# A gated cross-attention block on one core: moments and features of the score tiles handed to ScalarE and GpSimd

## The chip, the core and the metric

The kernel runs on one core of one Trainium2 chip. A core has TensorE (PE in the profile), VectorE (DVE), ScalarE (ACT), GpSimd (POOL) and the queue engine SyncE (SP), each with an instruction stream of its own that runs strictly in order; they meet only at semaphores. The metric is the device time of one launch in microseconds, the median of several runs.

## The reference

The inputs are x and a context, both (8, 512, 512) in float32. For each of the 8 batches the block computes an attention with 16 heads of width 32, whose temperature is computed from the scores themselves, and then a feed-forward part with quantised weights and activations:

```
Q, K, V = LN(x) @ Wq.T + bq, ctx @ Wk.T + bk, ctx @ Wv.T + bv        # 16 heads
scores  = Q K^T / sqrt(32)
mean_sim = mean(scores); max_sim = mean over rows of max(scores)
entropy_proxy = mean over rows of var(softmax(scores), ddof=1)
t    = exp(clip(MLP([mean_sim, max_sim, entropy_proxy])))              # one per head
attn = softmax(Q K^T / (2 t)) V
x    = x + tanh(g0) * (attn @ Wo.T + bo)
x    = x + tanh(g1) * (quant(gelu(quant(LN(x)) @ quant(W1).T)) @ quant(W2).T)
```

So the scores of a head are needed twice: once for the three features (called pass A below), and once, divided by the temperature, for the attention itself (pass B).

## The kernel before, in words

**Tiles.** A batch has 16 heads x 4 row blocks = 64 score tiles of 128 x 512 in pass A. Tile k belongs to head k // 4 and row block k % 4. Each goes through four steps: TensorE makes the scores in one of four PSUM banks (`a_ps`, `score_a`, L1471); VectorE takes minus the row maximum (`nmax`, `row_max`, L1007); ScalarE takes the exponential into one of three buffers (`etile`, `first_exp`, L778); VectorE takes the moments of that with a BN_STATS instruction (`stat`, `row_stat`, L1017), two tiles later. TensorE may write tile k when the exponential of tile k - 4 is done. For a few tiles of the first and of the last turn that has a pass A (`by_act`), ScalarE makes the moments: its exponential also sums the row (an accumulator read follows), and a Square with a sum (`square`, L788) follows the next exponential; VectorE then leaves out its BN_STATS for this tile and completes the six numbers of `stat` later (`stats_by_act`).

**Turns.** `body(i, par)` runs for i = -1 to 8; i = 1 to 6 are a loop of three passes over two bodies. In such a turn the core works on three batches at once: pass A of batch i, pass B and the feed-forward part of batch i - 1, and the projections K, V and Q of batch i + 1. Within a turn the order of the stages on every engine is the same:

1. the score section: 16 sets of pass B with 40 of the 64 pass-A tiles between them;
2. the four K products (`split_product`, 12 matmuls each, into the banks `b_ps0`, `b_ps1`, `o_ps`, `z_ps`), then the four products with Wo ("W"), the turned x ("X"), three V products, and the four Q products. The 24 remaining pass-A tiles stand beside these. How many stand where is written out in `A_PLAN`: the tuple has 16 places, four each for K, W, V and Q;
3. the features of pass A (`features`, on VectorE: sums and differences over `stat`, a reciprocal, and reductions over `nmax`, 12 small instructions), and the feed-forward part: the up products in row blocks t (`up`, L1650), Gelu by ScalarE (`gelus`, L940), the row maximum and the quantisation by VectorE (`scale_h`, L1218, and `quantise_h`, L1235), the turn of the quantised rows by TensorE (`turn`, L1661), half of which VectorE takes out of PSUM (`turned_h`, L1244), and the down products (L1685). After the up products of block 2 TensorE multiplies the features (L1720, L1724).

Four PSUM banks are taken in rotation by all products; `take` waits until the bank's last content has been taken out.

**What couples K and W.** ScalarE takes each K product out of its bank twice (`qk_out`: L847 with a sum, L851 in float16), after the exponentials of the pass-A tiles that stand beside this product. GpSimd then makes the float16 remainder of K product n (`split_qk(n)`, L684), and behind the one of n = 1 it scales and splits the last quarter of the attention's result (`split_y`: L640, L643, L645), whose last step signals `y_done`. TensorE waits for `y_done` before the first W product.

Of the kernel before, what the change touches and what calls it, by code (L numbers as in the profile page):

```python
# [22 lines left out]
ALU = mybir.AluOpType  # L23
# [43 lines left out]
BY_ACT = {b: sum(by_act(b, k) for k in range(H * T)) for b in (0, 7)}  # L67
# [3 lines left out]
LINKS_END = 12  # L71
LOWEST = -3.0e38
BIAS_STEPS = 5
SETUP_STEPS = G4 + 6
# [108 lines left out]
def nth(b, per, k):  # L183


    return (b + 1) * per + k
# [37 lines left out]
def flamingo_kernel(nc, x, ctxT, g_xattn, g_ffn, WqT, bq, WkT, bk, WvT, bv, WoT, bo,  # L224
                    w1T, b1, w2T, b2, w3T, b3, f1T, f2T, out):
    with ExitStack() as ctx:
# [3 lines left out]
        def sem(name):  # L230
            return ctx.enter_context(nc.semaphore(name))
# [58 lines left out]
        qmask = sb("qmask", [P, G4])  # L290
# [113 lines left out]
        qk_lo_done = per_batch("qk_lo_done", 2 * C)  # L404
        m_link = per_batch("m_link", LINKS_M)
        feat_done = per_batch("feat_done", 1)
        logt_done = per_batch("logt_done", 1)
        expt_done = per_batch("expt_done", 1)
        inv2t_done = per_batch("inv2t_done", 1)
# [3 lines left out]
        def slot_of(n):  # L413
            return (n % G4) * C + n // G4
# [171 lines left out]
        def _(pool):  # L586
            pool_waits = Waits(pool, stood)
            for s, events in per.values():
                pool.sem_inc(s, events)
            pool.sem_inc(out_done, 16 * T)  # L590
            for n in range(UNUSED):
                pool.sem_inc(mm_full[n], 1)
                pool.sem_inc(mm_free[n], 1)
# [78 lines left out]
            def from_cin(n):  # L672
                return cin[:, n % 2, :]


            def body(i, par):
# [65 lines left out]
        def _(act):  # L742
# [37 lines left out]
                                     accum_out=stat[:, at, 1:2] if by_act(b, k) else None).then_inc(a_exp, 1)  # L780

            def squares_by(b, k):
                return (BY_ACT[0] if b > 0 else 0) + sum(by_act(b, n) for n in range(k + 1))

            def square(b, k):
                at = slot_of(k // T) * T + k % T
# [197 lines left out]
        def _(dve):  # L984
            dve_waits = Waits(dve, stood)
            vec = nc.vector
# [30 lines left out]
                vec.bn_stats(stat[:, slot_of(k // T) * T + k % T, :], etile[:, k % E_SLOTS, :]).then_inc(a_stat, covered)  # L1017

            def stats_by_act(i):
                if i == 0:  # L1020
                    by_tile = stat[:, :, :].rearrange("p (g c t) f -> p g c t f", g=G4, t=T)
                    own = by_tile[:, :, 1:3, T - 1, :]
                else:
                    by_tile = stat[:, :, :].rearrange("p (h t) f -> p h t f", t=T)
                    own = by_tile[:, 2 * C - 1::C, :, :]
                mean, mean_too, rest = (own[:, :, :, f] for f in (1, 4, 5))
                links = 2 if i > 0 else 0
                dve_waits.wait_ge(squared, BY_ACT[0] + (BY_ACT[7] if i > 0 else 0))
                vec.tensor_scalar(mean, mean, 1.0 / S, None, ALU.mult).then_inc(act_link, 1)
                dve_waits.wait_ge(act_link, links + 1)  # L1030
# [3 lines left out]
                dve_waits.wait_ge(act_link, links + 2)  # L1034

            def tile_a(b, k, looked=False):

# [26 lines left out]
            def features(b, par):  # L1064
# [242 lines left out]
            def body(i, par):  # L1307
# [473 lines left out]
```

## Time and profile before

| | |
|---|---|
| median of 3 runs | 1333.83 us (1332.42 to 1334.48) |
| profiled execution, device time | 1336.35 us |
| its span, first to last instruction | 1334.5 us |
| mean granted TensorE clock | 0.969 |
| busy: PE / DVE / ACT / POOL | 89% / 82% / 71% / 30% of the span |
| chain that ended last, by engine | PE 49%, DVE 26%, issue 10%, ACT 8% |

The turns i = 1 to 7 end, by the temperature's last step on VectorE, at 316.4, 469.5, 623.7, 776.8, 930.8, 1083.9 and 1221.7 us. So a turn of the loop is 153.1 to 154.2 us long, and the six of them repeat one pattern. In the turn that ends at 623.7 us the score section runs to 539.8 us, the K products to 552, W to 564, X and V to 576, Q to 590, and the feed-forward part from 590. A row of the timeline gives the start and the duration in us, the engine and line, the tiles, and in brackets how long the engine had been idle before, and for whom it had waited. Durations of neighbouring instructions overlap in their last 0.1 us, so the pitch from start to start is what an engine needs for each.

### The profile page before, as it was taken

The numbers are of one execution on the slowest core, as the hardware profiler recorded it, in microseconds if no ns is written. First come the engines' busy times: TensorE is split into PE (matmuls) and PEld (weight loads), VectorE is DVE, ScalarE is ACT, GpSimd is POOL, SyncE is SP. The second block draws the span as 40 slices with busy tenths as digits, with TensorE's granted clock in tenths as the row PEclk, the third lists the DMA queues.
The fourth block names the chain that finished last, engine by engine and source line by source line (L and its number), as shares of the span: only waits on it lengthen the run. The fifth ranks groups of instructions, "written<-read, shape, count | busy, mean of one in ns | idle before, by whom it ended". The sixth has DMA issues, their size and how long they took to land.

```text
span 1334.5 us, 23561 instructions
## 1 busy us (share of the span) xinstructions
PE 1186.8 (89%) x6684; PEld 439.0 (33%) x6684; DVE 1093.2 (82%) x2049; ACT 941.7 (71%) x1593; POOL 396.3 (30%) x387
## 2 busy tenths in 40 slices
PE   4866598989999999998999999999989899869988
PEld 2322221444134422444124431344214441224234
DVE  7789689896998869896998869897898979985256
ACT  4688598576985689575985669665985669765833
POOL 3138555311452024510353124510353101100120
PEclk9969799999999999999999999999999999979989
DMA  8722211221112221211112221102112210001000
GB/s 305 224 75 64 55 41 49 48 48 58 35 39 48 57 74 48 49 38 42 50 48 48 55 76 49 28 21 65 64 49 48 48 65 1 1 0 47 18 0 32
DMA packets 36049, 73.70 MB, mean 55 GB/s; under 512 B 8144, under 2 KB 8528, under 8 KB 35408
## 3 DMA queue, kind: packets, MB, share of 16 engines
q1 hardware_dynamic: 35920, 72.13, 18.8%
q8 instruction: 62, 1.02, 0.3%
q14 instruction: 67, 0.55, 0.1%
HBM read 38.39 MB, written 8.39 MB: 35 GB/s over the span
## 4 chain that ended last, share of the span: by engine, by line
PE 49%; DVE 26%; issue 10%; ACT 8%; SPq 2%; DMA 1%; DVEq 1%; ACTq 0%; POOL 0%; POOLq 0%
PE b_ps L1445 10%; DVE stat L1017 7%; PE o_ps L1685 6%; DVE nmax L1007 5%; PE o_ps L1490 4%; ACT region L810 4%; PE o_ps L1445 4%; PE b_ps L1477 4%; PE a_ps L1471 4%; PE z_ps L1445 3%; ACT etile L778 2%; DVE hmax L1218 2%; PE z_ps L1685 2%; PE z_ps L1501 2%; PE b_ps L1650 2%
## 5 line engine op out<-in xcount | busy, mean ns | idle before, releaser
L778 ACT ACTIVATE etile<-a_ps,nmax 128x512 f32<-128x512 f32 x512 | 369.1, 734 | 104.3 <-DVE nmax L1007 104.1
L810 ACT ACTIVATE region<-b_ps,inv2t 128x512 f32<-128x512 f32 x512 | 354.8, 758 | 50.0 <-PE b_ps L1477 46.1
L1007 DVE TENSOR_REDUCE nmax<-a_ps 128x1 f32<-128x512 f32 x512 | 345.9, 679 | 53.7 <-PE a_ps L1471 49.7
L1017 DVE BATCH_NORM_STATS2 stat<-etile 128x6 f32<-128x512 f32 x492 | 335.5, 685 | 15.5 <-ACT etile L778 15.2
L1471 PE MATMUL a_ps<-kst,qst 96*128 96x512 f16 x512 | 198.1, 390 | 32.1 <-ACT etile L778 25.5
L1477 PE MATMUL b_ps<-qst,kst 97*128 97x512 f16 x512 | 192.8, 389 | 23.6 <-DVE region L1244 7.7
L1490 PE MATMUL o_ps<-region,vbuf 128*32 128x512 f32 x1024 | 137.2, 608 | 10.9 <-ACT region L810 7.1
L1477 PEld LDWEIGHTS b_ps<-qst,kst 97*128 97x128 f16 x512 | 49.2, 96 | 290.4 <-ACT region L810 259.3
L1501 PE MATMUL z_ps<-region,ones 128*32 128x512 f32 x1024 | 136.2, 604 | 8.4 <-DVE region L1054 8.4
L684 POOL TENSOR_TENSOR region<-region 128x512 f16<-128x512 f32 x64 | 79.8, 1249 | 208.9 <-ACT region L851 208.9
L640 POOL TENSOR_TENSOR region<-region 128x512 f32<-128x512 f32 x32 | 40.9, 1280 | 285.4 <-DVE region L1061 285.4
L1218 DVE TENSOR_REDUCE hmax<-region 128x1 f32<-128x512 f32 x128 | 81.7, 680 | 12.1 <-ACT region L940 10.9
L613 POOL CAST c_hi<-cin 128x512 f16<-128x512 f32 x28 | 17.1, 611 | 243.8 <-DMA cin<-in_ctxT_dram 243.0
L1685 PE MATMUL o_ps<-f,region 128*128 128x512 fp8e4 x352 | 79.6, 379 | 0.0
L1650 PE MATMUL b_ps<-f,region 128*128 128x512 fp8e4 x256 | 65.1, 394 | 15.2 <-DVE region L1244 12.1
L1471 PEld LDWEIGHTS a_ps<-kst,qst 96*128 96x128 f16 x512 | 50.7, 99 | 80.7 <-ACT etile L778 44.9
L940 ACT ACTIVATE region<-b_ps,xmax 128x512 f32<-128x512 f32 x64 | 43.3, 689 | 27.9 <-PE b_ps L1650 27.6
L661 POOL TENSOR_SCALAR cin<-cin,mv,rstd 128x512 f32<-128x512 f32 x28 | 58.1, 2081 | 2.8 <-POOL rstd L652 2.6
L950 ACT ACTIVATE region<-b_ps 128x1024 f16<-128x1024 f16 x31 | 31.7, 1023 | 31.6 <-PE b_ps L1661 30.8
L1051 DVE TENSOR_SCALAR region<-o_ps 128x512 f32<-128x512 f32 x32 | 21.8, 681 | 37.0 <-PE o_ps L1490 37.0
L650 POOL TENSOR_SCALAR rstd<-mv 128x2 f32<-128x2 f32 (+1 forms) x25 | 5.8, 232 | 139.0 <-DVE mv L1367 52.5
L1685 PEld LDWEIGHTS o_ps<-f,region 128*128 128x128 f16 x352 | 33.8, 98 | 38.1 <-issue 1.1
(313 smaller groups left out, 1989.9 us busy)
## 6 DMA issues: line engine op xcount, KB each, us to landing
kst<-region SPq DMA_DIRECT2D x96, 128.0 KB, 2.3
qst<-region SPq DMA_DIRECT2D x84, 128.0 KB, 2.3
xres<-in_x_dram SPq DMA_DIRECT2D x8, 1024.0 KB, 6.1
out_dram<-xres SPq DMA_DIRECT2D x32, 256.0 KB, 2.0
cin<-in_ctxT_dram SPq DMA_DIRECT2D x30, 256.0 KB, 2.7
cin<-in_x_dram SPq DMA_DIRECT2D x28, 256.0 KB, 2.6
kst<-in_f1T_dram SPq DMA_DIRECT2D x2, 1024.0 KB, 11.5
qst<-in_f2T_dram SPq DMA_DIRECT2D x2, 1024.0 KB, 9.0
```

Source lines behind the costliest of these rows:

```text
L778: nc.scalar.activation(etile[:, k % E_SLOTS, :], a_ps[k % A_BANKS][:, :], ACT.Exp, bias=nmax[:, slot_of(n), t:t + 1], scale=1.0, accum_out ...
L810: nc.scalar.activation(probs[:, (s + 1) % 2, g, :], b_ps[g % 2][:, :], ACT.Exp, scale=inv2t[:, slot:slot + 1]).then_inc(b_exp, 1)
L1007: vec.tensor_reduce(nmax[:, slot_of(k // T), k % T:k % T + 1], a_ps[k % A_BANKS][:, :], AX.X, ALU.max, negate=True).then_inc(a_max, 1)
L1017: vec.bn_stats(stat[:, slot_of(k // T) * T + k % T, :], etile[:, k % E_SLOTS, :]).then_inc(a_stat, covered)
L1218: ins = vec.tensor_reduce(hmax[:, n:n + 1], hbuf[t % 2][:, n * S:(n + 1) * S], AX.X, ALU.max, apply_absolute_value=True)
L1445: ins = mat(mm_ps[bank_n][:, :], left[l](c), right[r](c), start=(c, l, r) == pairs[0], stop=bias is None and (c, l, r) == pairs[-1])
L1471: mat(a_ps[k % A_BANKS][:, :], qst[par][0:SHIFT, slot, t * P:(t + 1) * P], kst[par][0:SHIFT, slot, :], start=True, stop=True).then_inc(a_f ...
L1477: mat(b_ps[g % 2][:, :], kst[par][0:SHIFT + 1, slot, k * P:(k + 1) * P], qst[par][0:SHIFT + 1, slot, :], start=True, stop=True).then_inc(b ...
L1490: ins = mat(o_ps[g * DK:(g + 1) * DK, :], vbuf[par][:, k, n * DK:(n + 1) * DK], probs[:, (s + 1) % 2, g, :], start=k == 0, stop=k == T - 1)
L1501: ins = mat(z_ps[g * DK:(g + 1) * DK, :], ones32[:, 0:DK], probs[:, (s + 1) % 2, g, :], start=k == 0, stop=k == T - 1)
L1650: ins = mat(mm_ps[bank_n][:, :], xqT[:, c, t * P:(t + 1) * P], f1[:, c, n * S:(n + 1) * S], start=c == 0, stop=c == C - 1)
L1685: ins = mat(mm_ps[bank_n][:, :], hT[t % 2][:, k, :], f2[:, k, :], start=k == 0, stop=k == KC - 1)
```

## The change

Four things are edited:

- `A_PLAN`, the places of 24 pass-A tiles in turns 1 to 6: K gets 3, 3, 2, 2 instead of 2, 2, 2, 2; W gets 2, 1, 1, 1 instead of 1, 1, 1, 1; V gets 0, 0, 0, 1 instead of 1, 1, 1, 1; Q keeps 2, 2, 2, 2.
- In turns 1 to 6 ScalarE makes the moments of the odd row blocks of heads 10 and 11, that is of tiles 41, 43, 45 and 47, all of which stand beside the K products.
- In turns 1 to 7 the features are made by GpSimd in 13 linked steps, but for the reciprocal, which stays on VectorE (`inverse_total`). Two steps (the total of `stat` and its square) stand ahead of the last `split_qk`, the rest behind it. The products of the sums of Q and K and the completion of ScalarE's moments stand ahead of the remainders of Q.
- The first turn keeps its plan and its features on VectorE; turn 7 keeps its plan.

```diff
-A_PLAN = (40, (2, 2, 2, 2, 1, 1, 1, 1, 1, 1, 1, 1, 2, 2, 2, 2))
+A_PLAN = (40, (3, 3, 2, 2, 2, 1, 1, 1, 0, 0, 0, 1, 2, 2, 2, 2))
+BY_ACT_HEADS = (10, 11)
 def by_act(i, k):
-    return isinstance(i, int) and (i == 0 and k % T == T - 1 and C <= k // T < 3 * C or i == 7 and k >= H * T - 3 * T)
+    n, row = k // T, k % T
+    if isinstance(i, int) and i == 0:
+        return row == T - 1 and C <= n < 3 * C
+    if isinstance(i, int) and i == 7:
+        return n >= H - 3
+    return n in BY_ACT_HEADS and row % 2 == 1
...
+            def stats_by_act(i):
...
+                mean, mean_too, rest = (own[:, :, :, f] for f in (1, 4, 5))
+                pool_waits.wait_ge(squared, nth(i, BY_ACT[1], count))
+                pool.tensor_scalar(mean, mean, 1.0 / S, None, ALU.mult).then_inc(act_pool, 1)
...
+                pool.tensor_copy(mean_too, mean)
+                pool.tensor_tensor(rest, mean, mean, ALU.mult).then_inc(act_pool, 1)
...
+                pool.tensor_scalar(rest, rest, -float(S), None, ALU.mult).then_inc(act_pool, 1)
...
+            def feature_total(b, c):
+                total = mstep[:, 0, :]
+                pool_waits.wait_ge(a_stat, nth(b, H * T, H * T))
+                if isinstance(b, int) and b == 7:
+                    stats_by_act(b)
+                c.link(pool.tensor_tensor(total, stat[:, :, 1], stat[:, :, 4], ALU.add))
+                c.link(pool.tensor_tensor(total, total, total, ALU.mult))
+            def feature_rest(b, c):
...
+                c.link(pool.tensor_tensor(some, nmax[:, :, 0:2], nmax[:, :, 2:4], ALU.add))
+                c.link(pool.tensor_tensor(feat[:, 1, :], some[:, :, 0], some[:, :, 1], ALU.add))
+                c.link(pool.tensor_tensor(diff, stat[:, :, 1], stat[:, :, 4], ALU.subtract))
+                c.link(pool.tensor_tensor(diff, diff, diff, ALU.mult))
...
+                pool_waits.wait_ge(inv_done, nth(b, 1, 1))
+                c.link(pool.tensor_tensor(square, square, inv, ALU.mult))
...
+                pool.tensor_tensor(feat[:, 2, :], some[:, :, 0], some[:, :, 1], ALU.add).then_inc(feat_done, 1)
...
-                if has_p:
-                    for n in range(C, 2 * C):
-                        split_qk(n)
+                if has_a and has_b:
+                    c = Chain(pool_waits, pool_link, LINKS_POOL, i)
+                    feature_products(i, par, c)
+                for n in range(C, 2 * C) if has_p else ():
+                    if has_a and has_b and n == 2 * C - 1:
+                        feature_total(i, c)
+                    split_qk(n)
+                if has_a and has_b:
+                    if not has_p:
+                        feature_total(i, c)
+                    feature_rest(i, c)
...
+            def inverse_total(b):
+                dve_waits.wait_ge(pool_link, nth(b, LINKS_POOL, 4))
+                vec.reciprocal(mstep[:, 3, :], mstep[:, 0, :]).then_inc(inv_done, 1)
...
-                if has_a and isinstance(i, int) and i == 7:
-                    stats_by_act(i)
-                if has_a:
+                if has_a and has_b:
+                    inverse_total(i)
+                elif has_a:
                     features(i, par)
```

ScalarE in turn 1, from the last exponential but one ahead of the first K product's exit to the second K product's exit; `b_ps0` and `b_ps1` hold the two products, `etile,stat<-` is an exponential or a square that also sums. Before:

```order
L778 ACTIVATE etile<-a_ps3,nmax 128x512
L778 ACTIVATE etile<-a_ps0,nmax 128x512
L118 ISA
L847 ACTIVATE region2,qksum0<-b_ps0,bqk 128x512
L851 ACTIVATE region2<-b_ps0,bqk 128x512
L778 ACTIVATE etile<-a_ps1,nmax 128x512
L778 ACTIVATE etile<-a_ps2,nmax 128x512
L847 ACTIVATE region2,qksum0<-b_ps1,bqk 128x512
L851 ACTIVATE region2<-b_ps1,bqk 128x512
```

The same place of the changed kernel:

```order
L862 ACTIVATE etile<-a_ps3,nmax 128x512
L862 ACTIVATE etile<-a_ps0,nmax 128x512
L862 ACTIVATE etile,stat<-a_ps1,nmax 128x512
L128 ISA
L932 ACTIVATE region2,qksum0<-b_ps0,bqk 128x512
L936 ACTIVATE region2<-b_ps0,bqk 128x512
L862 ACTIVATE etile<-a_ps2,nmax 128x512
L873 ACTIVATE etile,stat<-etile 128x512
L862 ACTIVATE etile,stat<-a_ps3,nmax 128x512
L862 ACTIVATE etile<-a_ps0,nmax 128x512
L873 ACTIVATE etile,stat<-etile 128x512
L932 ACTIVATE region2,qksum0<-b_ps1,bqk 128x512
L936 ACTIVATE region2<-b_ps1,bqk 128x512
```

Ahead of the second K product's exit there are now two more exponentials and two squares; one of the exponentials stands ahead of the first exit.

VectorE after the last pass-A tile of the same turn, with the row maxima of the first feed-forward block (`hmax<-region4`) at the end. Before:

```order
L1017 BN_STATS stat<-etile 128x6
L1069 TENSOR_TENSOR mstep<-stat 128x64
L118 ISA
L1070 TENSOR_TENSOR mstep<-stat 128x64
L1071 TENSOR_TENSOR mstep<-mstep 128x64
L1072 TENSOR_TENSOR mstep<-stat 128x64
L1073 SCALAR_TENSOR_TENSOR mstep<-mstep 128x64
L1075 TENSOR_TENSOR mstep<-mstep 128x64
L1076 RECIPROCAL mstep<-mstep 128x64
L1077 TENSOR_TENSOR mstep<-mstep 128x64
L1078 TENSOR_TENSOR qkprod<-qksum1 128x4
L1079 TENSOR_TENSOR feat<-qkprod,qmask 128x16
```

Three more rows (L1082, L1083 and the first L1218) follow there. In the changed kernel:

```order
L1102 BN_STATS stat<-etile 128x6
L1102 BN_STATS stat<-etile 128x6
L128 ISA
L1170 RECIPROCAL mstep<-mstep 128x64
L1303 TENSOR_REDUCE hmax<-region4 128x1
```

Eleven of the twelve instructions have left VectorE, and the one that stays waits for two steps of GpSimd.

GpSimd behind the remainder of the third Q product (`region1<-region2,region1` is such a remainder) in the changed kernel; before, the last remainder followed the third at once and nothing followed it:

```order
L760 TENSOR_TENSOR region1<-region2,region1 128x512
L128 ISA
L725 TENSOR_TENSOR mstep<-stat 128x64
L726 TENSOR_TENSOR mstep<-mstep 128x64
L760 TENSOR_TENSOR region1<-region2,region1 128x512
L734 TENSOR_TENSOR mstep<-nmax 128x32
L735 TENSOR_TENSOR feat<-mstep 128x16
L736 TENSOR_TENSOR mstep<-stat 128x64
L737 TENSOR_TENSOR mstep<-mstep 128x64
L739 TENSOR_SCALAR mstep<-mstep 128x64
L740 TENSOR_TENSOR mstep<-stat 128x64
L743 TENSOR_TENSOR mstep<-mstep 128x64
```

Three more steps (L745, L747 and L748) end the chain.

## Rows read from the trace of the kernel before

**Rows 1.** Timeline of TensorE, third turn of the loop: first instruction of the W products.
```profile
552.16 0.39 PE L1471 MATMUL a_ps<-kst,qst 96*128 96x512 f16 x1
```

**Rows 2.** Timeline of GpSimd, same turn, from the second K remainder on.
```profile
547.54 1.16 POOL L684 TENSOR_TENSOR region<-region 128x512 f16<-128x512 f32 x1 [1.81 <-ACT region L851]
548.65 1.27 POOL L640 TENSOR_TENSOR region<-region 128x512 f32<-128x512 f32 x1
...
550.78 1.16 POOL L645 TENSOR_TENSOR region<-region 128x512 f16<-128x512 f32 x1
```

**Rows 3.** Timeline of TensorE in the feed-forward part of the same turn.
```profile
600.72 1.07 PE L1661 MATMUL b_ps<-ident,region 128*128 128x128 f16 x16 [0.20 <-DVE region L1235]
...
606.01 1.02 PE L1650 MATMUL b_ps<-f,region 128*128 128x512 fp8e4 x4 [1.63 <-DVE region L1244]
```

**Rows 4.** Timeline of VectorE, same turn, from the last moments to the quantisation.
```profile
589.83 1.87 DVE L1017 BATCH_NORM_STATS2 stat<-etile 128x6 f32<-128x512 f32 x3
...
592.35 1.07 DVE L1071 TENSOR_TENSOR mstep<-mstep 128x64 f32<-128x64 f32 x1
...
595.93 2.46 DVE L1218 TENSOR_REDUCE hmax<-region 128x1 f32<-128x512 f32 x4
...
599.31 1.29 DVE L1235 TENSOR_SCALAR region<-region,hsc 128x2048 f32<-128x2048 f32 x1
```

**Rows 5.** Timeline of ScalarE beside the K products, same turn.
```profile
542.55 0.69 ACT L778 ACTIVATE etile<-a_ps,nmax 128x512 f32<-128x512 f32 x1 [3.35 <-DVE nmax L1007]
543.13 0.68 ACT L847 ACTIVATE region<-b_ps,bqk 128x512 f32<-128x512 f32 x1
...
544.37 0.69 ACT L778 ACTIVATE etile<-a_ps,nmax 128x512 f32<-128x512 f32 x1
...
546.11 0.68 ACT L847 ACTIVATE region<-b_ps,bqk 128x512 f32<-128x512 f32 x1
...
546.77 0.69 ACT L851 ACTIVATE region<-b_ps,bqk 128x512 f16<-128x512 f32 x1
```

**Rows 6.** Timeline of ScalarE in turn 7: exponentials and a square that sum.
```profile
1167.14 0.68 ACT L778 ACTIVATE etile<-a_ps,nmax 128x512 f32<-128x512 f32 x1
...
1167.81 0.62 ACT L788 ACTIVATE etile<-etile 128x512 f32<-128x512 f32 x1
...
1168.42 0.68 ACT L778 ACTIVATE etile<-a_ps,nmax 128x512 f32<-128x512 f32 x1
```

**Rows 7.** Timeline of VectorE beside the K products, third turn: two row maxima.
```profile
542.95 0.67 DVE L1007 TENSOR_REDUCE nmax<-a_ps 128x1 f32<-128x512 f32 x1
...
545.93 0.67 DVE L1007 TENSOR_REDUCE nmax<-a_ps 128x1 f32<-128x512 f32 x1
```

**Rows 8.** One turn earlier, VectorE: the row maximum of tile 41.
```profile
388.52 0.68 DVE L1007 TENSOR_REDUCE nmax<-a_ps 128x1 f32<-128x512 f32 x1
```

**Rows 9.** One turn earlier, ScalarE: the second exit of the second K product.
```profile
392.57 0.68 ACT L851 ACTIVATE region<-b_ps,bqk 128x512 f16<-128x512 f32 x1
```

**Rows 10.** The chain that ended last, in order of time: start us, us, what.
```profile
541.50 0.22 PE a_ps L1471
```

**Rows 11.** Timeline of ScalarE, third turn: the first Gelu.
```profile
593.28 0.69 ACT L940 ACTIVATE region<-z_ps,xmax 128x512 f32<-128x512 f32 x1
```

**Rows 12.** Timeline of GpSimd, third turn: a small step, and the last Q remainder.
```profile
567.15 0.24 POOL L650 TENSOR_SCALAR rstd<-mv 128x4 f32<-128x4 f32 x1 [8.75 <-DVE mv L1367]
...
592.04 1.30 POOL L684 TENSOR_TENSOR region<-region 128x512 f16<-128x512 f32 x1 [1.88 <-ACT region L851]
```

**Rows 13.** Timeline of ScalarE in turn 7: the last Gelu of block 1.
```profile
1199.12 0.69 ACT L940 ACTIVATE region<-z_ps,xmax 128x512 f32<-128x512 f32 x1 [0.17 <-PE z_ps L1650]
```

**Rows 14.** Timeline of VectorE in turn 7: the step behind the maxima of block 1.
```profile
1201.24 0.16 DVE L1221 TENSOR_REDUCE hsc<-hmax 128x1 f32<-128x4 f32 x1
```

**Rows 15.** Timeline of TensorE in turn 0: the restart after a gap.
```profile
102.41 0.39 PE L1471 MATMUL a_ps<-kst,qst 96*128 96x512 f16 x1 [2.50 <-ACT etile L778]
```

**Rows 16.** Busy time by stretch: us, PE, PEld, DVE, ACT, POOL, granted clock, DMA share, GB/s.
```profile
112.00:116.00 4.00, 4.00 (x13) 1.45 (x12) 4.00 (x6) 2.73 (x7) 4.00 (x3) 0.62 0.92 207
```

More of the change, by code:

```diff
@@ L59 @@
 EARLY = A_BANKS
+BY_ACT_HEADS = (10, 11)
 def by_act(i, k):
-    return isinstance(i, int) and (i == 0 and k % T == T - 1 and C <= k // T < 3 * C or i == 7 and k >= H * T - 3 * T)
-BY_ACT = {b: sum(by_act(b, k) for k in range(H * T)) for b in (0, 7)}
+    n, row = k // T, k % T
[4 more added lines that the diff above has]
+    return n in BY_ACT_HEADS and row % 2 == 1
+BY_ACT = {b: sum(by_act(b, k) for k in range(H * T)) for b in (0, 1, 7)}
+assert BY_ACT[0] == 2 * BY_ACT[1]
 assert all(sets + sum(dense) == H * T for sets, dense in (A_PLAN_0, A_PLAN, A_PLAN_7))
@@ L71 @@
 LINKS_END = 12
+LINKS_POOL, LINKS_ACT = 13, 3
 LOWEST = -3.0e38
@@ L406, in flamingo_kernel @@
         feat_done = per_batch("feat_done", 1)
+        pool_link, inv_done, act_pool = sem("pool_link"), sem("inv_done"), sem("act_pool")
         logt_done = per_batch("logt_done", 1)
@@ L590, in _ @@
             pool.sem_inc(out_done, 16 * T)
+            pool.sem_inc(pool_link, 2 * LINKS_POOL)
+            pool.sem_inc(inv_done, 2)
+            pool.sem_inc(act_pool, 2 * LINKS_ACT)
             for n in range(UNUSED):
@@ L673, in from_cin @@
                 return cin[:, n % 2, :]
+            def stats_by_act(i):
+                by_tile = stat[:, :, :].rearrange("p (h t) f -> p h t f", t=T)
+                if isinstance(i, int) and i == 7:
+                    own, count = by_tile[:, 2 * C - 1::C, :, :], BY_ACT[7]
+                else:
+                    first, second = (slot_of(n) for n in BY_ACT_HEADS)
+                    own, count = by_tile[:, first:second + 1:second - first, 1::2, :], BY_ACT[1]
+                mean, mean_too, rest = (own[:, :, :, f] for f in (1, 4, 5))
+                pool_waits.wait_ge(squared, nth(i, BY_ACT[1], count))
+                pool_waits.stand()
+                pool.tensor_scalar(mean, mean, 1.0 / S, None, ALU.mult).then_inc(act_pool, 1)
+                pool_waits.wait_ge(act_pool, nth(i, LINKS_ACT, 1))
+                pool_waits.stand()
+                pool.tensor_copy(mean_too, mean)
+                pool.tensor_tensor(rest, mean, mean, ALU.mult).then_inc(act_pool, 1)
+                pool_waits.wait_ge(act_pool, nth(i, LINKS_ACT, 2))
+                pool_waits.stand()
+                pool.tensor_scalar(rest, rest, -float(S), None, ALU.mult).then_inc(act_pool, 1)
+                pool_waits.wait_ge(act_pool, nth(i, LINKS_ACT, 3))
@@ new lines, in feature_products @@
+            def feature_products(b, par, c):
+                pool_waits.wait_ge(qk_done, nth(b, 2 * C, 2 * C))
+                c.link(pool.tensor_tensor(qkprod[:, :], qksum[par][:, 0:C], qksum[par][:, C:2 * C], ALU.mult))
+                c.link(pool.tensor_tensor(feat[:, 0, :].rearrange("p (g c) -> p g c", g=G4),
+                                          qkprod[:, :].unsqueeze(1).broadcast_to([P, G4, C]),
+                                          qmask[:, :].unsqueeze(2).broadcast_to([P, G4, C]), ALU.mult))
+                if not (isinstance(b, int) and b == 7):
+                    stats_by_act(b)
@@ new lines, in feature_total @@
+            def feature_total(b, c):
+                total = mstep[:, 0, :]
+                pool_waits.wait_ge(a_stat, nth(b, H * T, H * T))
+                if isinstance(b, int) and b == 7:
+                    stats_by_act(b)
+                c.link(pool.tensor_tensor(total, stat[:, :, 1], stat[:, :, 4], ALU.add))
+                c.link(pool.tensor_tensor(total, total, total, ALU.mult))
+            def feature_rest(b, c):
+                total, diff, square, inv = (mstep[:, k, :] for k in range(4))
+                by_tile = square.rearrange("p (h t) -> p h t", t=T)
+                pool_waits.wait_ge(a_max, nth(b, H * T, H * T))
+                some = diff[:, 0:2 * H].rearrange("p (h t) -> p h t", t=2)
+                c.link(pool.tensor_tensor(some, nmax[:, :, 0:2], nmax[:, :, 2:4], ALU.add))
+                c.link(pool.tensor_tensor(feat[:, 1, :], some[:, :, 0], some[:, :, 1], ALU.add))
+                c.link(pool.tensor_tensor(diff, stat[:, :, 1], stat[:, :, 4], ALU.subtract))
+                c.link(pool.tensor_tensor(diff, diff, diff, ALU.mult))
+                pool_waits.stand()
+                c.link(pool.tensor_scalar(diff, diff, S / 4.0, None, ALU.mult))
+                pool.tensor_tensor(square, stat[:, :, 2], stat[:, :, 5], ALU.add).then_inc(pool_link, 1)
+                c.n += 1
+                pool_waits.wait_ge(pool_link, c.base + c.n)
+                c.link(pool.tensor_tensor(square, square, diff, ALU.add))
+                pool_waits.wait_ge(inv_done, nth(b, 1, 1))
+                c.link(pool.tensor_tensor(square, square, inv, ALU.mult))
+                some = total[:, 0:2 * H].rearrange("p (h t) -> p h t", t=2)
+                c.link(pool.tensor_tensor(some, by_tile[:, :, 0:2], by_tile[:, :, 2:4], ALU.add))
+                pool.tensor_tensor(feat[:, 2, :], some[:, :, 0], some[:, :, 1], ALU.add).then_inc(feat_done, 1)
+                c.end()
@@ L782, in squares_by @@
             def squares_by(b, k):
-                return (BY_ACT[0] if b > 0 else 0) + sum(by_act(b, n) for n in range(k + 1))
+                own = sum(by_act(b, n) for n in range(k + 1))
+                return own if isinstance(b, int) and b == 0 else nth(b, BY_ACT[1], own)
             def square(b, k):
@@ L1019, in stats_by_act @@
             def stats_by_act(i):
[L1020 to L1025, printed above, removed]
+                by_tile = stat[:, :, :].rearrange("p (g c t) f -> p g c t f", g=G4, t=T)
+                own = by_tile[:, :, 1:3, T - 1, :]
                 mean, mean_too, rest = (own[:, :, :, f] for f in (1, 4, 5))
-                links = 2 if i > 0 else 0
-                dve_waits.wait_ge(squared, BY_ACT[0] + (BY_ACT[7] if i > 0 else 0))
+                dve_waits.wait_ge(squared, BY_ACT[0])
                 vec.tensor_scalar(mean, mean, 1.0 / S, None, ALU.mult).then_inc(act_link, 1)
-                dve_waits.wait_ge(act_link, links + 1)
+                dve_waits.wait_ge(act_link, 1)
                 vec.tensor_copy(mean_too, mean)
```

2 lines of the change are left out of this document (1 added, 1 removed).

## The prediction

> **What bounds the kernel now.** I read the chain by engine first (PE 49%, DVE 26% of the span), then the waits of TensorE, then the timelines of one loop turn, engine by engine. Six turns repeat one pattern and make up most of the span, so whatever the change does counts six times, and once more in turn 7. In the stretch from the K products to the Q products TensorE issues almost without a gap, and the chain runs along it. VectorE and ScalarE matter there only where TensorE stands still. Two places of the turn are of interest.
>
> The first is the start of the W products at 552.16 [rows 1]. TensorE could not start them before `y_done`, and GpSimd's last step for it ended at 550.78 + 1.16 = 551.94 [rows 2], 0.22 earlier. So this chain is the one that ends last already now, with nothing to spare: ScalarE's second exit of the second K product (546.77 [rows 5]), the remainder at 547.54, the scaling at 548.65, the split to 551.94. The reader should see in rows 2 and 5 that GpSimd starts 0.77 after that ScalarE instruction starts, and was idle before.
>
> The second is the feed-forward part. TensorE waits 0.20 for the first quantised block and 1.63 for the bank that VectorE empties at L1244 [rows 3]. VectorE gets there late since it runs the twelve feature instructions from 591.7 (589.83 + 1.87) to 595.93 before its first maximum of the feed-forward part [rows 4], though the first Gelu is out at 593.28 + 0.69 = 593.97 [rows 11].
>
> **What is gained: the features leave VectorE.** What stays is the reciprocal, behind two GpSimd steps over 64 columns. The trace has no such step. Its nearest rows are 0.24 us for 4 columns and 1.30 us for 512 columns [rows 12]. Between them lies some 0.35, nearer to the small one by its columns; with a link of 0.1 the two steps take 0.9 and the reciprocal, estimated at 0.6 from the 4.2 us that twelve instructions take, ends at about 593.3. That is ahead of the Gelu, so the maxima start at 594.0 instead of 595.93: 1.93 earlier. At the upper end, 1.4 a step, the reciprocal would end at 595.1 and the gain be 0.8; at the lower, 0.25 a step, nothing more is gained, since the Gelu is then last. Everything VectorE does from there to L1244 is its own queue, so the bank comes free up to 1.93 earlier, and TensorE, which idled 0.20 + 1.63 = 1.83 (a little more with the overlap of the rows), can use practically all of it. What is late next is TensorE itself, which has no gap then up to the last turned block. A further bit is lost, because the ten steps of `feature_rest` (ten times 0.45 us from about 594 on, to 598.5) run beside VectorE's first quantisation. The instruction L1071 took 1.07 us [rows 4], and ended when GpSimd's remainder that had begun at 592.04 ended (593.34 [rows 12]); the other feature instructions of its size are far shorter, as the whole chain of twelve takes 4.2. So a VectorE instruction can be held until a GpSimd step ends; one or two such holds of up to 0.35 lie in the path, and I take off 0.23. Gain: 1.7 us a turn, with 0.8 and 1.93 as ends.
>
> Advanced Engine Details and Errata of the Trainium skill, in VectorE Performance Modes, says that GpSimd instructions and VectorE instructions in a two-port mode block each other. The 1.07 us of L1071 agrees with it, and it speaks against this part of the change: before, one GpSimd instruction stood beside the features, now ten stand beside the maxima and the quantisation. By that rule each quantisation that falls into the chain waits at most for the rest of one step, which leaves the sum as it is.
>
> `feat_done` itself is not needed before TensorE's products with the features, right behind the instruction at 606.01 (604.1 then), 5.6 us after the estimated end of the chain. The last Q remainder moves behind the two steps, some 0.7 later; the loads that it releases on the SyncE queue are needed by the engines only some ten us later. In turn 7 the gain is smaller, for there the last Gelu of block 1 ends at 1199.12 + 0.69 = 1199.81 [rows 13]; one maximum (0.69) behind it lets the next step start at 1200.55 instead of 1201.24 [rows 14]: 0.65 gained. The four GpSimd steps for ScalarE's moments that stand ahead there are hidden by this.
>
> **What is lost: ScalarE beside the K products.** Up to the end of the second K product's exit ScalarE has now two more exponentials and two squares with a sum, one of the exponentials ahead of the first exit. Counted out, the pitches are a plain exponential 0.58 (542.55 to 543.13), a K product's exit 1.24 (543.13 to 544.37), its first half 0.66 (546.11 to 546.77) [rows 5]; an exponential with a sum 0.67, a square with a sum 0.61 [rows 6]. The exponential of tile 40 stays at 542.55, as VectorE's maximum sets it. That of tile 41 may start 0.81 after its maximum (542.95 [rows 7]; the same distance that tile 40's has), at 543.76, and must now be done ahead of the first exit: the exit starts at 543.76 + 0.67 = 544.43 and ends at 545.67. Then 0.58 + 0.61 + 0.67 + 0.58 + 0.61 = 3.05 bring the second exit to 548.72 (the maximum of tile 43, at 545.93 [rows 7], is in time, since the moments of tile 41 have left VectorE). Its second half starts at 549.38 instead of 546.77: 2.6 later. One turn earlier the same count from 388.52 [rows 8] gives 389.33 + 0.67 + 1.24 + 3.05 + 0.66 = 394.95, against 392.57 [rows 9]: 2.4 later. The turns alternate between the two patterns, so 2.5 on average. GpSimd, and with it `y_done`, follows by the full amount, since it was idle before the remainder. W starts 2.5 later in each turn. TensorE would be done with the K products at about 552.4, two tiles later than now, and stands still for 2.3 us.
>
> Part of this comes back at once. A tile costs TensorE 0.22 [rows 10]. Behind the start of W it now has one tile more in W and three fewer in V; the two that went to K are done in time that would be idle. That is 2 x 0.22 = 0.43 saved. The four BN_STATS that leave VectorE, at 0.6 each, lie beside TensorE's products and gain nothing; neither does the quantisation of x, which has no tiles in front of it any more and finishes some 2 us earlier, long before TensorE turns it. ScalarE has caught up by the third W product, where it had idled.
>
> The lower end of the loss is 2.1, if the squares overlap more than in turn 7; the upper 3.0, if GpSimd meets the port of VectorE on the way.
>
> **Sum.** A turn: 2.5 - 0.43 - 1.7 = +0.37 us; six turns +2.2; turn 7 -0.65. Together +1.6 us. The profiled execution took 1336.35 us, its span 1334.5 and 1.85 around it; it becomes 1337.9. The median of the runs shown is 1333.83, so I expect 1335.4 there. A change of under 0.2% (2.7 us) is about what a measurement of this kernel cannot tell from none.
>
> **The rivals.** *Faster, A:* the delay at W does not come. ScalarE's order is written, so for that `y_done` would have to be released by something else, or the K products' exits wait less than I count. For it speaks that ScalarE idles 3.35 us ahead of 542.55 [rows 5]; against it that this wait is for VectorE's maximum, and cannot be used. The time would be 6 x (-1.7 - 0.2) - 0.65, that is -12 us: 1322. If only half of the delay comes, it is 1328.
>
> *Slower, B:* the GpSimd chain is slow. Its place is `inverse_total`: VectorE stands at it until GpSimd has done two steps, and behind it are all maxima. At the 1.4 us a step of the upper end the gain falls from 1.7 to 0.8, which costs 6 x 0.9 = 5.4 us more: 1341. If ten such steps end after TensorE needs the features, it waits again: 593.9 + 14 = 608 against 604, another 6 x 4 = 24. It decides from 1.0 us a step on. Against it: the small step of 0.24 us [rows 12].
>
> *Slower, C:* TensorE's clock. The new gap at W is 2.3 us. After a gap of 2.50 us in turn 0 TensorE restarted with 0.39 us a matmul, its fast level of 2.4 GHz [rows 15]; but after further gaps close by the granted clock was 0.62 over 4 us [rows 16], a loss of 0.38 x 4 = 1.5 us at 1.2 GHz. In each turn that would be 6 x 1.5 = +9: 1344. Against it: TensorE is busy without a gap for 12 us on both sides.
>
> **How the numbers follow.** Forecast (both terms as counted, within about 4 us) 0.60; A in whole or part 0.20; B 0.12; C 0.08. The forecast's own range is 1331.5 to 1340: the terms' ends are 2.1 - 0.43 - 1.93 = -0.26 a turn and 3.0 - 0.43 - 1.3 = +1.27. The whole range reaches to half of A and to C's foot: 1327 to 1342. Of the forecast's 0.60, 0.05 is faster by over 0.2%, 0.33 within, 0.22 slower. With A 0.20 faster but for 0.02, and B and C slower but for 0.02, that is faster 0.24, same 0.37, slower 0.39.
>
> **What the profile after must show.** TensorE ahead of the first W product: a gap of about 2.3 us in each of the six turns, and GpSimd's L684 equivalent for the second K product some 2.5 us later against the start of K. TensorE's 1.63 us wait for VectorE's turned block: down to under 0.4. The maxima of block 0 directly behind the first Gelu. GpSimd's steps over 64 columns: 0.3 to 0.4 us. The start of Q after the start of K: 2.1 us later. I am wrong if the W gap stays at 0.2, if steps take 1 us, or if the granted clock in the loop is under 1.00.

## The result

Slower by 0.39%: 1338.07 us median (1334.94 to 1340.72, 8 runs) against 1332.88 (1331.44 to 1334.48, 8 runs), ratio 1.0039, 95% interval 1.0027 to 1.005. On another chip it was 1336.54 (1333.16 to 1342.21, 12 runs) against 1333.09, ratio 1.0028 (1.0014 to 1.0041). The time lies in the predicted range, 2.7 us above the predicted value: +5.2 us were measured where +1.6 were forecast. The runs spread over 5.8 us instead of 3.0. The profiled execution took 1337.47 us (span 1335.7, granted clock 0.967).

### The profile page after: what moved, and what is told of

It reads as the page before. It is cut to its first block, busy times and chain, and to the rows that moved or that the text cites. A ratio compares the mean times of both kernels' runs of the same rounds, so it can differ in the third digit from the quotient of the medians.

```text
span 1335.7 us, 23792 instructions
## 1 busy us (share of the span) xinstructions
PE 1187.1 (89%) x6684; PEld 438.9 (33%) x6684; DVE 1059.5 (79%) x1945; ACT 957.2 (72%) x1665; POOL 433.3 (32%) x513
## 4 chain that ended last, share of the span: by engine, by line
PE 46%; DVE 23%; issue 12%; ACT 11%; SPq 3%; POOL 2%; DMA 2%; DVEq 1%; ACTq 1%; POOLq 0%
PE b_ps L1530 8%; DVE stat L1102 6%; PE o_ps L1770 6%; DVE nmax L1092 6%; PE o_ps L1575 4%; ACT region L895 4%; PE b_ps L1562 4%; PE o_ps L1530 4%; ACT etile L862 3%; PE z_ps L1530 3%; PE a_ps L1556 3%; PE b_ps L1735 2%; PE z_ps L1770 2%; PE z_ps L1586 2%; PE b_ps L1746 2%
## 5 line engine op out<-in xcount | busy, mean ns | idle before, releaser
L1102 DVE BATCH_NORM_STATS2 stat<-etile 128x6 f32<-128x512 f32 x468 | 318.4, 683 | 19.7 <-ACT etile L862 19.4
L760 POOL TENSOR_TENSOR region<-region 128x512 f16<-128x512 f32 x64 | 76.3, 1192 | 196.7 <-ACT region L936 195.3
```

## The profile after

Timeline of TensorE, third turn, the first instruction of the W products, the same place as [rows 1]. The square brackets hold the idle time ahead of it and what ended it.
```profile
555.34 0.39 PE L1556 MATMUL a_ps<-kst,qst 96*128 96x512 f16 x1 [2.13 <-POOL region L659]
```
The gap that was forecast as 2.3 us is 2.13 here and 1.97 in every second turn. GpSimd in the same turn, against [rows 2]: both K remainders, then the scaling and the last step of the split.
```profile
546.42 1.16 POOL L760 TENSOR_TENSOR region<-region 128x512 f16<-128x512 f32 x1 [5.60 <-ACT region L936]
550.70 1.16 POOL L760 TENSOR_TENSOR region<-region 128x512 f16<-128x512 f32 x1 [3.12 <-ACT region L936]
551.82 1.28 POOL L654 TENSOR_TENSOR region<-region 128x512 f32<-128x512 f32 x1
...
553.96 1.16 POOL L659 TENSOR_TENSOR region<-region 128x512 f16<-128x512 f32 x1
```
GpSimd idles 3.12 us for ScalarE, makes the second remainder, and only then starts on y, whose input VectorE had ready at 546.60. ScalarE, against [rows 5]:
```profile
543.12 0.69 ACT L862 ACTIVATE etile<-a_ps,nmax 128x512 f32<-128x512 f32 x1 [3.35 <-DVE nmax L1092]
544.31 0.69 ACT L862 ACTIVATE etile<-a_ps,nmax 128x512 f32<-128x512 f32 x1 [0.50 <-DVE nmax L1092]
...
549.91 0.71 ACT L936 ACTIVATE region<-b_ps,bqk 128x512 f16<-128x512 f32 x1
```
From the first exponential to the second exit's second half it takes 6.79 us, where it took 4.22.

The feed-forward part of the third turn, VectorE first, against [rows 4].
```profile
592.54 1.87 DVE L1102 BATCH_NORM_STATS2 stat<-etile 128x6 f32<-128x512 f32 x3
595.28 0.55 DVE L1170 RECIPROCAL mstep<-mstep 128x64 f32<-128x64 f32 x1 [0.87 <-POOL mstep L726]
596.71 2.46 DVE L1303 TENSOR_REDUCE hmax<-region 128x1 f32<-128x512 f32 x4 [0.87 <-ACT region L1025]
...
600.10 1.29 DVE L1320 TENSOR_SCALAR region<-region,hsc 128x2048 f32<-128x2048 f32 x1
```
Twelve feature instructions have become one reciprocal, and the maxima wait for the first Gelu and no longer for the features. GpSimd beside it:
```profile
594.49 0.38 POOL L725 TENSOR_TENSOR mstep<-stat 128x64 f32<-128x64 f32 x1 [1.62 <-DVE stat L1102]
594.95 0.29 POOL L726 TENSOR_TENSOR mstep<-mstep 128x64 f32<-128x64 f32 x1
...
600.26 1.20 POOL L748 TENSOR_TENSOR feat<-mstep 128x16 f32<-128x16 f32 x1
```
A step over 64 columns takes 0.29 to 0.39 us. Next, the row of the up-projections in the page of the profile, first after the change and then before it. Behind the bar stand busy us, mean ns of one, and the idle us ahead of them with what ended most of it:
```profile
L1735 PE MATMUL b_ps<-f,region 128*128 128x512 fp8e4 x256 | 64.7, 392 | 6.1 <-DVE region L1329 3.3
```
```profile
L1650 PE MATMUL b_ps<-f,region 128*128 128x512 fp8e4 x256 | 65.1, 394 | 15.2 <-DVE region L1244 12.1
```
The wait for the block that VectorE turns out of PSUM [rows 3] has gone from 12.1 us in all to 3.3.

What the prediction gave too little weight shows in the windows of 8 us from the start of W. The last three numbers of a row are the granted clock, the DMA share and GB/s. First and third turn after:
```profile
246.00:254.00 8.00, 7.65 (x28) 3.18 (x29) 4.53 (x7) 4.37 (x9) 5.81 (x7) 0.79 0.43 98
...
555.00:563.00 8.00, 7.67 (x36) 3.50 (x37) 5.72 (x9) 4.37 (x9) 5.81 (x7) 1.00 0.36 82
```
In the first turn TensorE started 28 matmuls instead of 36 and ran at 1.2 GHz for a part of the window (0.21 x 8 = 1.7 us lost). That is called a fall of the clock below. In the other five windows after the change, and in all six before it, the clock was 1.00.

All traces are read by three distances, each worked out from TensorE's timeline as a mean over the six loop turns, in us. "K to W" goes from the first matmul of the K products to the first of the W products (one score tile, 0.22 us, behind the row shown above), "W to up" from there to the first up-projection, over the turns without a fall, and "up to features" from there to the transpose of the features. "Falls" counts the falls of the clock between W and up, out of six. The runs were made on several chips; the kernel before, run beside each group, measured 1332.9 to 1333.4.
```
                          K to W   W to up   falls   up to features   median us
before                     12.34     37.95      0        16.57        1332.9 to 1333.4
after                      14.82     37.48      1        14.77        1338.07
after, second trace        14.82     37.48      0        14.76        1336.54
features alone             12.34     37.93      0        14.63        1320.26
tiles, moments alone       14.82     37.48      4        16.58        1352.18
  and the gap filled       14.83     37.48      0        16.54        1346.53
tiles and features         14.62     37.47      2        14.63        1332.60
after, gap filled          14.82     37.48      0        14.76        1333.21
after, y first             12.61     37.48      0        14.76        1320.07
before, y first            12.12     37.95      0        16.57        1332.48
features, y first          12.12     37.93      0        14.63        1319.09
after, y first, again      12.61     37.47      0        14.75        1320.54
features, y first, again   12.12     37.93      0        14.62        1318.68
```

## Experiments

**The features alone, and the rest alone.** The first run takes back the tile plan and ScalarE's moments in the loop (lines that follow from these are left out):
```
-A_PLAN = (40, (3, 3, 2, 2, 2, 1, 1, 1, 0, 0, 0, 1, 2, 2, 2, 2))
+A_PLAN = (40, (2, 2, 2, 2, 1, 1, 1, 1, 1, 1, 1, 1, 2, 2, 2, 2))
-    return n in BY_ACT_HEADS and row % 2 == 1
+    return False
```


> The features on GpSimd as in the changed kernel, with the tiles where they were before and no moments on ScalarE in the loop turns. My theory: the two halves of the change are independent. The feed-forward part starts 1.8 us earlier in six turns (the changed kernel's trace has TensorE's features' transpose 14.6 to 14.9 us behind the first up-projection instead of 16.5), and the start of W keeps its 0.2 us gap. 1332.9 - 11 = 1322 us. The rival, that the moved tiles are what made room at the feed-forward part (less queued on VectorE ahead of it), has hardly a gain here: 1331 to 1333.

1320.26 us (1317.32 to 1322.12), ratio to before 0.9895 (0.9876 to 0.9914). The distance from up to features falls by 1.94 a turn, and 6 x 1.94 = 11.6 of the 13.1 us gained. So the room at the feed-forward part doesn't come from the moved tiles, as the rival had it.

The second run leaves the plan and the moments and gives VectorE its features back (the part on VectorE; GpSimd's steps for the features are taken out as well):
```
-                if has_a and has_b:
-                    inverse_total(i)
-                elif has_a:
+                if has_a and has_b:
+                    dve_waits.wait_ge(act_pool, nth(i, LINKS_ACT, 3))
+                if has_a:
                     features(i, par)
```


> The tiles and ScalarE's moments as in the changed kernel (GpSimd still finishes those moments), but all features back on VectorE. My theory: it pays the delay at W, 6 x (2.5 - 0.46) = 12 us, and gains nothing: 1345 us, and 1 to 6 us more if TensorE loses its clock after some of the gaps at W. The rival: the 1.6 us wait ahead of the last quantised blocks hides part of the delay, 1338 or less.

1352.18 us (1349.92 to 1354.82, 4 runs), ratio 1.0138 (1.0116 to 1.016), 18.8 us over the kernel before. The turn's distances give 6 x (2.48 - 0.47) = 12 us. Its trace has four falls of the clock behind W, 1.7 us each, which would be the other 6.8; the mean granted clock of its four runs, 0.964 against 0.9695 in the 15 beside it of the kernel before, agrees. Windows of 8 us from W in its six turns, two of them left out:
```profile
245.00:253.00 8.00, 7.71 (x28) 3.19 (x29) 4.53 (x7) 4.32 (x9) 5.75 (x7) 0.79 0.43 99
402.00:410.00 8.00, 7.93 (x29) 3.28 (x30) 4.53 (x7) 4.10 (x9) 5.53 (x6) 0.79 0.47 108
560.00:568.00 8.00, 7.40 (x35) 3.37 (x36) 5.46 (x9) 4.63 (x10) 6.07 (x7) 1.00 0.23 51
715.00:723.00 8.00, 7.30 (x26) 2.98 (x27) 4.53 (x7) 4.74 (x10) 6.16 (x7) 0.79 0.40 91
```
The wait ahead of the last turned block is still there in full (12.6 us in all), so it hid none of the delay.

**What holds W.** One step of GpSimd's order is moved, in the changed kernel and in the one before:
```
                     if has_p:
                         split_qk(n)
-                    if has_b and n == 1:
+                    if has_b and n == 0:
                         split_y(i - 1, C - 1)
```


> The changed kernel with one step moved on GpSimd: the last split of y (scale, cast, remainder, about 3.3 us) stands ahead of the remainder of the second K product instead of behind it. My theory: only that order holds W up; its input is there at 546.6, the split ends at about 551.0 in the third turn instead of 555.1, TensorE is through with the K products at 553.2 and has no gap. 6 x 2.05 = 12.3 us less than the changed kernel's 1338, and no clock loss: 1324 us or a little less. The rival: the second K product's remainder becomes late by 0.3 to 3 us and the K exits on ScalarE, which wait for remainders, hold TensorE instead; then half of it or less, 1332 to 1338.

The changed kernel so reordered took 1320.07 us, ratio to before 0.9891 (0.9872 to 0.991), some 16 to 18 below the changed kernel. GpSimd in its third turn:
```profile
538.42 1.16 POOL L760 TENSOR_TENSOR region<-region 128x512 f16<-128x512 f32 x1 [5.61 <-ACT region L936]
539.55 1.26 POOL L654 TENSOR_TENSOR region<-region 128x512 f32<-128x512 f32 x1
...
541.67 1.16 POOL L659 TENSOR_TENSOR region<-region 128x512 f16<-128x512 f32 x1
542.79 1.16 POOL L760 TENSOR_TENSOR region<-region 128x512 f16<-128x512 f32 x1
545.81 1.15 POOL L760 TENSOR_TENSOR region<-region 128x512 f16<-128x512 f32 x1 [1.87 <-ACT region L936]
```
and TensorE's first tile of W, with no idle time ahead of it:
```profile
545.04 0.38 PE L1556 MATMUL a_ps<-kst,qst 96*128 96x512 f16 x1
```
The split is over at 542.83, 2.2 us before W starts; the second K remainder comes right behind it, and nobody waits for that. K to W falls by 2.21 of the 2.48 us, so it was this order that passed ScalarE's delay on to W: y had been ready, and GpSimd stood idle waiting for a K exit. The 0.27 that stay are about the work of the two more tiles (2 x 0.22 us, less the 0.2 that TensorE had waited there before).

> The kernel before with the same step moved: the last split of y ahead of the remainder of the second K product. The gap ahead of W in the kernel before is 0.2 us, so by my theory there is little to gain: 6 x 0.2 = 1.2 us, 1331.7. If it gained several us, TensorE would have been waiting there for something that the rows did not show.

1332.48 us, ratio 0.9991 (0.9981 to 1.0001), a difference that can't be told from none; K to W fell by 0.22, and the wait there was 0.2. By the distances this order cost the kernel before about 1 us, and the changed one 6 x 2.21 = 13 us and the falls of the clock.

**What the gap does to the clock.** The changed kernel was run again, beside one in which nine matmuls fill the gap:
```
                 elif has_b:
+                    bank_n = take(i, "W", 0)
+                    for n in range(9):
+                        mat(mm_ps[bank_n][:, :], ones16[:, :], bias16[:, 1, :], start=True, stop=True)
                     pe_waits.wait_ge(y_done, nth(i - 1, C, C))
```


> The changed kernel once more, beside the next three on one chip. 1338 us, within 1335 to 1341, with TensorE at half its clock for about 3.4 us behind some of the six gaps at W (one in the first trace, which cost its turn 1.7 us).

> The changed kernel with nine extra matmuls of 128x512 (0.22 us each, 2.0 us together) on TensorE ahead of its wait for y_done, written to the bank of the first W product, which overwrites them. W cannot start earlier, so nothing is gained by the order; only the gap is filled. My theory: the turns as such add about 1 us over the kernel before, and the rest of the 5 us is TensorE's clock falling after the gap in some turns, 1.7 us each time; filled, the time is 1334.5 (1333 to 1336) with a smaller spread, and no turn has the half clock at W. The rival: the clock falls there for another reason or the rest is something else, and the time stays at 1338.

Unfilled 1336.54 us (1333.16 to 1342.21) and filled 1333.21 (1331.4 to 1334.81), ratios to before 1.0028 (1.0014 to 1.0041) and 1.0001 (0.9992 to 1.0009): the intervals don't meet. W starts where it did in the turn, behind nine more matmuls:
```profile
550.61 2.11 PE L1659 MATMUL b_ps<-bias,ones 128*128 128x512 f16 x9
552.91 0.39 PE L1556 MATMUL a_ps<-kst,qst 96*128 96x512 f16 x1 [0.19 <-POOL region L659]
```
More work on TensorE made the kernel 3.3 us faster and cut the spread from 9 us to 3.4. Of the unfilled runs the slowest had a granted clock of 0.964 over its span, the fastest 0.970. The means on this chip are 0.9672 over the twelve unfilled runs, 0.9701 over the eleven filled and 0.9695 over 29 of the kernel before. As an estimate, (1 - clock) x span gives 43.7, 39.8 and 40.6 us lost to the clock, and the spans without it are 1291.2, 1291.5 and 1290.6: what the filling gives back is clock.

> The kernel with the moved tiles and moments but all features on VectorE (1352.2 us, with the half clock at W in four of six turns of its trace), and nine extra matmuls of 128x512 in the gap ahead of W, written to a bank that the first W product overwrites. My theory: 6 x (2.5 - 0.46) = 12.2 us of the 18.8 over the kernel before are the delay, the rest the clock: filled, it takes 1345.3 us (1343.5 to 1347), and all six turns need 37.5 us from W to the first up-projection. The rival: the missing 6 us are in the feed-forward part or elsewhere, and the time stays above 1349.

1346.53 us (1343.23 to 1349.73, 4 runs), ratio 1.011 (1.0095 to 1.0126), with no fall in six turns. That is 13.6 us over the kernel before, where the unfilled one, on another chip, was 18.8 over it. Here the runs still spread over 6.5 us. Taken together the traces show 7 falls in the 24 turns with a gap of 1.7 to 2.1 us at W, none in 12 with the gap filled, and none at this place in the 42 turns whose gap is 0.2 us or less.

**Which part of ScalarE's work makes the delay.** This is the changed kernel with `return False` for the loop turns in `by_act`, its tile plan kept.

> The changed kernel with the moved tiles, but with no moments on ScalarE in the loop turns: VectorE makes them all. My theory: the squares and the sums are about half of the 2.5 us at W (2 x 0.61 + 2 x 0.09 = 1.4 us), the exponentials of the two tiles the rest; W starts 1.1 to 1.3 us late, the gap is below 1 us, and the clock does not fall: 6 x 1.35 + 4 = 12 us less than 1338: 1326. The rival: without the moments VectorE has two BN_STATS more (0.6 us each) ahead of the maxima, the exponentials wait for those, and W is as late as with the squares: 1338.

1332.6 us (1330.07 to 1333.14), ratio 0.999 (0.9981 to 0.9999): my expectation of 1326 was wrong, though the rival's 1338 was too. W came only 0.2 us sooner, and the trace has two falls behind it. ScalarE without the squares:
```profile
543.14 0.69 ACT L855 ACTIVATE etile<-a_ps,nmax 128x512 f32<-128x512 f32 x1 [0.51 <-DVE nmax L1085]
...
546.12 0.69 ACT L855 ACTIVATE etile<-a_ps,nmax 128x512 f32<-128x512 f32 x1 [0.47 <-DVE nmax L1085]
547.30 0.69 ACT L855 ACTIVATE etile<-a_ps,nmax 128x512 f32<-128x512 f32 x1 [0.50 <-DVE nmax L1085]
...
548.55 0.69 ACT L929 ACTIVATE region<-b_ps,bqk 128x512 f16<-128x512 f32 x1
```
The squares' time has turned into waits for VectorE's maxima, which stand behind BN_STATS again. So the moved tiles make the delay also without the moments, which take VectorE's part off and put it on ScalarE at nearly the same price; what the moments would do without the moved tiles was not run. Of the 3.9 us below the changed kernel on the same chip, 6 x 0.14 are up to features (14.63 in every turn) and 6 x 0.2 the start of W. The other 2 us agree with the clock of the runs, 0.9687 in the mean against 0.9672, but not with falls at W: the trace has two of them, and makes up for them in turn 7, which takes 3.3 us less from W to the features' transpose than in the second trace of the changed kernel.

**Does the place of the tiles matter without the gap?** This version has the features on GpSimd, the old plan and y first. It was run once, and then once more beside the changed kernel with y first.

> Features on GpSimd, tiles and moments as in the kernel before, and the last split of y ahead of the second K remainder. My theory: the gains add up, 1320.3 - 6 x 0.2 = 1319 us, the same within 1 us as the changed kernel with that order (1320.1), since with no gap at W it does not matter where the three tiles lie. The rival: the tiles' place is worth 6 x 0.46 = 2.8 us by itself, and this one stays at 1321 to 1323.

> The changed kernel with the last split of y first, again, beside the next kernel on one chip: 1320 us. With no gap at W the place of the three tiles should be worth nothing: TensorE does the same work between the start of K and the first up-projection (12.6 + 37.5 = 50.1 us against 12.2 + 37.9 = 50.1 in the other order).

> Features on GpSimd, tiles and moments as before, the last split of y first, again: 1319.5 us, 0.8 us (3 turns x 0.27) below the one beside it, as its feed-forward part takes 14.63 us in every turn and not 14.90 in every second. The rival: a difference of 2 us or more, which would make the tiles' place matter by itself.

First 1319.09 us, ratio 0.989 (0.9876 to 0.9905); then, on one chip, 1320.54 for the changed kernel with y first (ratio 0.99, 0.9885 to 0.9915) and 1318.68 for this one (0.9899, 0.9883 to 0.9915). A difference of 1.9 us between medians of four and five runs that spread over 4 and 5 us is no more than a sign, and the ratios are the same; the distances explain 6 x 0.15. So nothing shows that the tiles' place is worth anything by itself. This version has the lowest medians of those tried, 14 us under the kernel before, though not clearly below the features alone (1320.26) or the changed kernel with y first.

## Why the prediction was right, and where not

The sign and the range hold, and the two large terms were right in mechanism and size. The sum missed 3.6 of the 5.2 us, and the error is in the chance and form of rival C. The range was wide enough to hold it.

- *ScalarE beside the K products, +2.5 us a turn:* +2.48 (2.36 to 2.62 from turn to turn). The chain is the one named. The count was right, but the squares are not what it hangs on: without the two squares it is still 2.28, since VectorE's maxima then come late. The prediction took the maximum of tile 43 as in time because the moments of tile 41 had left VectorE, which is the other side of the same price.
- *Two tiles done in idle time, -0.43:* -0.47 from W to the first up-projection.
- *The features off VectorE, -1.7:* -1.80. TensorE's gain is 1.94 where the features alone move, the upper end named. From this 0.27 goes in every second turn of the changed kernel, by a hold like the one for which 0.23 was taken off. In the second turn, GpSimd's last step and VectorE's quantisation:
```profile
445.94 0.22 POOL L748 TENSOR_TENSOR feat<-mstep 128x16 f32<-128x16 f32 x1
```
```profile
446.04 1.29 DVE L1320 TENSOR_SCALAR region<-region,hsc 128x2048 f32<-128x2048 f32 x1 [0.30 <-DVE hsc L1310]
```
VectorE's instruction before had ended at 445.74, and the quantisation started 0.45 us after that one's start instead of 0.19 as in the third turn, and 0.10 behind the start of GpSimd's step. In the third turn the quantisation started first, and the same step of GpSimd took 1.20 us. Advanced Engine Details and Errata of the Trainium skill, in VectorE Performance Modes, says that GpSimd instructions and VectorE instructions in a two-port mode block each other. The 1.20 us agree with it, and so does the 0.26 us that VectorE came late, though no row names the port. Nor does a row say that L1071, whose 1.07 us the prediction took to agree with this rule, was in such a mode: they show a hold beside GpSimd and no more.
- *Turn 7, -0.65:* about -0.2. This term was mis-sized by 0.4. VectorE's first maxima stand 2.0 us earlier behind the first up-projection (7.37 instead of 9.35), but TensorE reaches the features' transpose only 0.47 earlier, and W starts 0.24 later. VectorE's step of [rows 14], 16.42 us behind the first up-projection before, comes at 15.94, that is 0.48 sooner and not 0.65: the last Gelu of block 1, which [rows 13] took as fixed, ends 0.2 later there (15.19 instead of 14.99), while TensorE's clock stays down a little longer (0.80 instead of 0.95 in the two us from 12 us behind the first up-projection). Why W of that turn comes 0.24 later, counted from turn 6's transpose, stays open.
- *The sum, +1.6:* the distances give 6 x (2.48 - 0.47 - 1.80) - 0.2 = +1.1, and with the gap filled the kernel measured +0.1 (+0.9 by the estimate without the clock's part). That this is so near to +1.6 is in part luck, since the small errors of the terms go both ways. The upper end of the range was added up with 1.3 for the features' gain, for which no row stands; with the 0.8 that the working names as its end it is 3.0 - 0.43 - 0.8 = 1.77 a turn, or about 1344 us. The measured time lies inside either way. The chances of faster, same and slower come to 0.23, 0.37 and 0.40 by their own terms, not 0.24, 0.37 and 0.39.
- *Rival C, chance 0.08, +1.5 us in each turn:* this is the step that failed. I weighed the clock as a case of all turns or none, and held against it that TensorE is busy for 12 us on both sides. It falls in some turns, 1.7 us each time. Filling the gap gave back 3.3 us, as much as two falls in six turns; the kernel's own two traces have one and none, so the two are worked out from the times and not counted. With the sum as forecast that makes 1.6 + 3.3 = 4.9 us, against 5.2 and 3.4 measured. As a term of the sum, 2 x 1.5 = 3 with the two known only from these runs, it would have made the forecast 1338.4. The prediction's own sign of being wrong, a granted clock under 1.00 in the loop, came in the first turn of the profiled execution.
- *Rivals A and B* fell: the delay came in full, and GpSimd's steps over 64 columns took 0.3 to 0.4 us, not 1.4.

## What to carry to other kernels

Before work is put ahead of an exit, follow who is queued behind it on the next engine: here GpSimd idled 3.12 us for a K exit with the input of a more urgent step already there. Swapping two steps of its order took 16 to 18 us off the changed kernel, while the moved tiles and moments gained nothing in any version. A gap on TensorE of about 2 us cost its own length and, in 7 of 24 turns, 1.7 us more at half clock; such a cost belongs into the sum by its expected share, and not among the rivals as a case of all or nothing. Change one thing at a time: the half that moved the features was worth 13 us, and the other half took all of it back and 5 us more.

## What the hardware showed

- The clock's falls aren't set by the gap's length alone: gaps of the same 2.13 and 1.97 us were followed by a granted clock of 0.79 over 8 us in four of six turns of one trace, one of six in another and none in a third. What tells them apart stays open.
- It also falls without any gap at W. In the second trace of the changed kernel with y first it did so in the third turn, behind the wait of the first row below ("issue": the engine waited for nothing that the profile shows). The K products began 1.8 us later in the turn than in the first trace of the same kernel:
```profile
473.77 0.43 PE L1562 MATMUL b_ps<-qst,kst 97*128 97x512 f16 x1 [1.65 <-issue]
```
```profile
474.00:482.00 8.00, 8.00 (x41) 1.63 (x43) 5.36 (x10) 6.85 (x12) 5.31 (x6) 0.79 0.37 111
```
- Every trace has two such waits in the loop, of 0.56 to 1.74 us. The clock fell behind three of these 26: 1.65 us here, 1.24 in the first trace of this kernel and 1.74 in the second of the features with y first. Waits of 1.44 and 1.58 us in other traces had none behind them. So part of the spread of every version, the kernel before too, may come from there.
- A GpSimd step over 128x16 took 0.22 us when it started ahead of VectorE's 128x2048 quantisation, and 1.20 us when the quantisation had started 0.16 us ahead of it.
